# Two-layer decoder on one core: fp32 foldings and ternary weights moved late, expert lanes moved, the experts' product turned, fewer products for bias and sums

## The reference, cut to what matters

```python
# layer 0
x = ln(x + (einsum('bes,st->bet', x, Wr + Wc) + bias))            # a mix over the last axis, with decay matrices
x = ln(x + cross_attention(x, ctx, Wq, Wkv_expand, Wout))
logits = x @ router_w; e = argmax(logits)                         # one of 8 experts for each token
xs = x * sigmoid(max(logits))
x = ln(x + (silu(xs @ gate_w[e]) * (xs @ up_w[e])) @ down_w[e] + shared_ffn(x))
# layer 1
x = ln(x + fft_attention(x, W_q, W_kv, W_o))
q_big = ((x @ Wq.T) per head) @ w_kc_q;  q_r = q_big @ W_qr;  k_r = kv_rope @ W_kr     # 16 heads
out = (softmax(q_r k_r) kv_rope @ w_kc_kv.T) @ Wo.T
x = ln(x + out)
gu = x @ ternary(w_gate_up).T; h = silu(gate) * up                # 2 x 1024 columns
x = ln(x + rms_norm(h) @ ternary(w_proj).T)
```

## Time and profile before

| | us |
|---|---|
| median of 3 runs (lowest, highest) | 703.32 (700.88, 707.11) |
| the profiled execution's own time | 706.16 |
| its span (first to last instruction) | 704.9 |
| instructions | 14612 |

### The profile page before, as it was taken

How to read it: one execution, slowest core, us unless ns; L and a number is a source line. 1 busy time by engine, 2 the same in 40 slices (tenths; PEclk the granted TensorE clock), 3 DMA queues, 4 the chain that set the end, 5 groups by cost and what they waited for, 6 DMA issues and landing times.

```text
span 704.9 us, 14612 instructions
## 1 busy us (share of the span) xinstructions
PE 595.1 (84%) x5393; PEld 460.6 (65%) x5393; DVE 503.4 (71%) x1297; ACT 408.1 (58%) x914; POOL 357.3 (51%) x405
## 2 busy tenths in 40 slices
PE   4888788998898775899267789999989999999996
PEld 3655566776666553555233578888768777978885
DVE  3766557776787787556279867777888879968475
ACT  2765456665677752444173356666675766578374
POOL 2435665765549870000398933264484543245565
PEclk9998899999999898999767799999999999999999
DMA  7642212423023422231501000001101010000001
GB/s 235 191 150 75 71 43 85 113 81 99 24 76 124 135 96 90 90 99 61 153 27 45 16 1 2 1 1 32 31 1 31 1 31 3 1 1 2 1 1 61
DMA packets 50416, 41.98 MB, mean 60 GB/s; under 512 B 15513, under 2 KB 48794, under 8 KB 50330
## 3 DMA queue, kind: packets, MB, share of 16 engines
q1 hardware_dynamic: 48810, 36.85, 17.7%
q0 software_dynamic: 1536, 4.20, 1.8%
HBM read 31.72 MB, written 10.35 MB: 60 GB/s over the span
## 4 chain that ended last, share of the span: by engine, by line
PE 42%; DVE 7%; ACT 5%; issue 4%; POOL 2%; DMA 0%; POOLq 0%; DVEq 0%; ACTq 0%
PE bank L1032 8%; PE bank L1034 7%; PE bank L1033 7%; PE bank L1450 6%; PE bank L1039 4%; PE bank L1214 3%; DVE wide L1763 1%; ACT wide L1589 1%; PE bank L1432 1%; PE bank L1315 1%; PE bank L1290 1%; PE bank L1317 1%; PE bank L1288 1%; PE bank L1287 1%; PE bank L1286 1%
## 5 line engine op out<-in xcount | busy, mean ns | idle before, releaser
L1763 DVE TENSOR_TENSOR first<-bank,first 128x512 f16<-128x512 f32 (+3 forms) x113 | 65.3, 592 | 19.4 <-ACT first L1656 6.3
L1039 PE MATMUL bank<-c_identity,wide 128*128 128x128 f32 (+2 forms) x267 | 46.4, 295 | 34.3 <-ACT wide L1589 17.8
L2220 POOL TENSOR_TENSOR first<-first 128x512 f16<-128x512 f32 x44 | 53.0, 1208 | 37.6 <-ACT first L1650 32.4
L1039 PEld LDWEIGHTS bank<-c_identity,wide 128*128 128x128 f32 (+2 forms) x267 | 32.7, 149 | 42.7 <-ACT wide L1589 19.2
L1763 DVE TENSOR_TENSOR wide<-bank,wide 128x512 f16<-128x512 f32 (+3 forms) x85 | 47.0, 566 | 16.1 <-ACT wide L1629 8.5
L1039 PE MATMUL bank<-c_identity,first 128*128 128x128 f32 (+2 forms) x297 | 48.2, 285 | 7.7 <-DVE first L1949 2.4
L2244 POOL DMA_INDIRECT wide<-made_rows,made_at x8 | 8.1, 1007 | 75.3 <-DMA made_rows<-wide 73.5
L1039 PEld LDWEIGHTS bank<-c_identity,first 128*128 128x128 f32 (+2 forms) x297 | 33.7, 140 | 15.3 <-DVE first L1949 3.0
L2200 POOL TENSOR_TENSOR first<-first,minus_half 128x2 f32<-128x2 f32 x30 | 21.5, 717 | 27.8 <-DVE first L1872 27.8
L1032 PE MATMUL bank<-wide,first 128*128 128x256 f16 (+3 forms) x115 | 28.1, 260 | 7.2 <-DVE first L1763 5.9
L2319 POOL TENSOR_TENSOR wide<-wide 128x512 f16<-128x512 f32 x16 | 18.0, 1124 | 31.2 <-ACT wide L1739 31.2
(11 more groups left out here) (509 smaller groups left out, 2249.0 us busy)
## 6 DMA issues: line engine op xcount, KB each, us to landing
wide<-in_L_xattn_Wq SPq DMA_DIRECT2D x9, 256.0 KB, 3.1
wide<-in_L_ffn_gate_w SPq DMA_DIRECT2D x8, 256.0 KB
wide<-in_L_ffn_up_w SPq DMA_DIRECT2D x8, 256.0 KB
wide<-in_L_ffn_down_w SPq DMA_DIRECT2D x8, 256.0 KB
wide<-in_L_xattn_Wo SPq DMA_DIRECT2D x16, 128.0 KB
wide<-in_L_ffn_w_gate_up SPq DMA_DIRECT2D x8, 256.0 KB
first<-in_x SPq DMA_DIRECT2D x7, 256.0 KB, 5.0
x_mid<-first SPq DMA_DIRECT2D x7, 256.0 KB, 3.2
```

Of the source, the lines that this page charges most:

```text
L1039: last = nc.tensor.transpose(view[0:m, c0:c0 + n], src, kc["identity" if dt == F32 else "identity_bf"][0:n, 0:n])
L1763: return V.tensor_tensor(lo, whole, hi, ALU.subtract)
L2220: G.tensor_tensor(B.pl[r], B.pf, B.ph[r], ALU.subtract).then_inc(says("ex_l"), 1)
```

## The change

1. `TURNS` is now e0 to e2, h0 to h3, e3 to e7, h4 to h7, and then the ternary stages in the order 0, 4, 1, 5, 2, 6, 3, 7. A unit of layer 1 waits for less at a time: `q` g for folding 2g + 1, `gu` g for stages g and g + 4, `proj` 2 and 3 for all.
2. The expert lanes leave the staging buffers: lanes 0 to 2 lie over layer 0's lane 3, lane 3 over the fifth, lanes 4 to 6 over lane 0. Each waits for the store of the unit that was there (`was_in`). The shared experts' weights and the layer 1 lanes move or shrink to make room.
3. `x_gu` takes the expert's weights as the stationary operand in blocks of 128 columns, so that gate and up come out turned, and `x_b`'s transposes go. `x_b_hi` and `x_b_lo` read `X.h` in SBUF.
4. The bias is one product of 128 rows instead of two of one row (`pm_b` prepares two rows, the rest zero). `rm` needs two products instead of four, since `ss` of the last group adds the two halves on POOL.
5. A folding: `hb` writes its two heads to output rows 0 to 63 and 64 to 127, head by head in turn; `hk` is one transpose, and `hc` two products with a block-diagonal `krT` instead of four.

```diff
-TURNS = [("e", e) for e in range(KEPT)] + [(kind, n) for n in range(NPREP) for kind in "hf"] + [("e", e) for e in range(KEPT, NE)]
+EARLY_FOLDS = 4
+TERNARY = [n // 2 + 4 * (n % 2) for n in range(NPREP)]
+TURNS = ([("e", e) for e in range(KEPT)] + [("h", n) for n in range(EARLY_FOLDS)] + [("e", e) for e in range(KEPT, NE)]
+         + [("h", n) for n in range(EARLY_FOLDS, NPREP)] + [("f", n) for n in TERNARY])
+def was_in(n):
+    return 3 if n < 3 else 4 if n == 3 else FIRST
...
-        if n < LANES:
-            gate += prepared
-        elif o is None:
-            gate += [("in_mid", FIRST - 2, 0), ("in_mid", FIRST - 1, 0)]
+        if o is None:
+            gate += [("in_mid", was_in(n), 0)]
...
-        chain("x_b", n, 0, [("x_h", n, 0)], k, pe=32, hi=38, lo=42)
+        p.add("x_b_hi", n, 0, "ACT", 38, [("x_h", n, 0)], k)
+        p.add("x_b_lo", n, 0, "DVE", 40, [("x_b_hi", n, 0)], k)
...
-            chain("q", u, g, [("turn_lo", u, 1), ("ho_lo", 0, NPREP - 1)], k, pe=136)
+            chain("q", u, g, [("turn_lo", u, 1), ("ho_lo", 0, 2 * g + 1)], k, pe=136)
...
-            p.add("gu", u, g, "PE", 180, [("turn_lo", u, 2)] + [("fw_c", 0, i) for i in range(NPREP)], k, 2, ("hf", u, g))
+            p.add("gu", u, g, "PE", 180, [("turn_lo", u, 2)] + [("fw_c", 0, i) for i in (g, g + 4)], k, 2, ("hf", u, g))
...
-        a = wide.back(stage_at + n * 5120) if n < LANES else fifth.back(6144) if n == LANES else couples[1].back(LANE0 + (n - LANES - 1) * 5120)
+        a = couples[1].back(LANE0 + n * 5120) if n < 3 else fifth.back(6144) if n == 3 else couples[0].back((n - 4) * 5120)
...
-        for n in range(HEADS):
-            for q in range(2):
-                last = mm(b[0:R, n * D:(n + 1) * D], W.qr[:, q, n, :], k.t1[:, n, q, :], start=(q == 0), stop=(q == 1))
+        for q in range(2):
+            for n in range(HEADS):
+                last = mm(b[n * R:(n + 1) * R, 0:D], W.qr[:, q, n, :], k.t1[:, n, q, :], start=(q == 0), stop=(q == 1))
...
-            for n in range(HEADS):
-                mm(b[:, (2 * c + n) * DC:(2 * c + n + 1) * DC], k.t2[:, n * D + c * P:n * D + (c + 1) * P], k.krT[:, n * DC:(n + 1) * DC],
-                   start=True, stop=True)
+            mm(b[:, c * P:(c + 1) * P], k.t2[:, c * P:(c + 1) * P], k.krT, start=True, stop=True)
...
-                    for half in range(2):
-                        last = mm(o, kc["all_ones"][0:1, :], k.bias[half], start=False, stop=(half == 1))
+                    last = mm(o, kc["all_ones"], k.bias, start=False, stop=True)
...
-        for c in range(C):
-            last = mm3(b[:, :], cut(X.xT, ALL, slice(c * P, (c + 1) * P)), tuple(w[:, c * 2 * D:(c + 1) * 2 * D] for w in gu), c == 0, c == C - 1)
+        for m in range(2 * C):
+            for c in range(C):
+                at = c * 2 * D + m * P
+                last = mm3(b[:, m * P:(m + 1) * P], tuple(w[:, at:at + P] for w in gu), cut(X.xT, ALL, slice(c * P, (c + 1) * P)), c == 0, c == C - 1)
...
-            for n in range(2):
-                last = mm(b[:, t:t + 1], B.ss[:, n * S + t * P:n * S + (t + 1) * P], k.one, start=(n == 0), stop=(n == 1))
+            last = mm(b[:, t:t + 1], B.ss[:, t * P:(t + 1) * P], k.one, start=True, stop=True)
...
+        if g == 3:
+            pool.step(last)
+            last = G.tensor_tensor(B.ss[:, 0:S], B.ss[:, 0:S], B.ss[:, S:2 * S], ALU.add)
```

More of the change, by code:

```diff
@@ L141 @@
               "fold_dve": ("hq_lo", "ho_lo"), "ternary_dve": ("f_sc", "f_gt"), "route_dve": ("rt_top", "rt_hot", "rk_seen", "rk_slot"), "gate_act": ("rt_gate", "rt_xs"), "table_dve": ("tb_cnt", "tb_tile", "tb_tok"),
-              "expert_pe": ("x_t", "x_gu", "x_b", "x_dn"), "expert_act": ("x_t_hi", "x_tan", "x_b_hi", "x_out"),
+              "expert_pe": ("x_t", "x_gu", "x_dn"), "expert_act": ("x_t_hi", "x_tan", "x_b_hi", "x_out"),
               "expert_dve": ("x_t_lo", "x_h", "x_b_lo")}
@@ L655, in program @@
     k.t1 = wide.tile([HEADS, 2, D], F32, 96)
[L656 removed]
+    k.t2 = wide.tile([D])
     k.t3 = wide.tile([2 * D])
[L658 removed]
+    k.krT = sb("krT", [P, P])[:]
     wide_end = wide.at
@@ L668, in program @@
     pre.dv = wide.tile([2])
-    pre.bias = wide.tile([S], F32, 1)
+    pre.bias, pre.rest = wide.tile([S], F32, 2), wide.tile([S], F32, 2)
     pre.ones32 = wide.tile([P])
@@ L758, in tile @@
             raise AssertionError("no room")
-        area = tile([4608])
+        area = tile([4096])
         def part(at, words, dt=F32):
@@ L860, in ld_mix @@
         load(pre.wrow, A["L0_attn_weight"][1:2, :].broadcast_to([P, S]), dma["mix"])
-        load(pre.bias, A["L0_attn_bias"].rearrange("(a n) -> a n", a=1), dma["mix"])
+        load(pre.bias, A["L0_attn_bias"].rearrange("(a n) -> a n", a=1).broadcast_to([2, S]), dma["mix"])
         for c in range(C):
@@ L1096, in hk @@
         W = k.W[k.stage_no["h", j] % 2]
-        flip(bank("hk", 0, j), [(n * DC, R, W.kr[:, n, :]) for n in range(HEADS)]).then_inc(says("hk"), 1)
+        flip(bank("hk", 0, j), [(0, P, W.kr.rearrange("p h n -> p (h n)"))]).then_inc(says("hk"), 1)
     def ha(u, j):
@@ L1208, in proj @@
         else:
+            for i in range(NPREP):
+                pe.wait_ge(*done("fw_c", 0, i))
             b = bank("proj", u, n)
@@ L1441, in gu @@
         pe.wait_ge(*done("turn_lo", u, 2))
-        for i in range(NPREP):
+        for i in (g, g + 4):
             pe.wait_ge(*done("fw_c", 0, i))
@@ L1464, in tensor_program @@
     parts = {f.__name__: f for f in (pm_mm, pt, pd, po, pb, hk, ha, hw, hb, hc, fw, turn, ctx, kv, proj, q, max, mt, sc, pv, ot, rt, rk, sh, tb,
-                                     x_t, x_gu, x_b, x_dn, ft, kt, cs, vt, gu, rm)}
+                                     x_t, x_gu, x_dn, ft, kt, cs, vt, gu, rm)}
     for name, u, g in k.plan.order["PE"]:
@@ L1542, in hk_c @@
         act.wait_ge(*done("hk", 0, j))
-        fn(k.krT, bank("hk", 0, j)[0:R, 0:HEADS * DC], ACT.Copy).then_inc(says("hk_c"), 1)
+        act.wait_ge(*done("pm_pow", 0))
+        for n in range(HEADS):
+            own = slice(n * R, (n + 1) * R)
+            last = fn(k.krT[own, n * DC:(n + 1) * DC], bank("hk", 0, j)[own, 0:DC], ACT.Copy)
+        last.then_inc(says("hk_c"), 1)
     def ha_c(u, j):
@@ L1556, in hb_c @@
         act.wait_ge(*done("hb", 0, j))
-        fn(k.t2, bank("hb", 0, j)[0:R, :], ACT.Copy).then_inc(says("hb_c"), 1)
+        fn(k.t2, bank("hb", 0, j)[:, 0:D], ACT.Copy).then_inc(says("hb_c"), 1)
     def hq_hi(u, j):
@@ L1692, in x_b_hi @@
     def x_b_hi(n, g):
-        act.wait_ge(*done("x_b", n))
-        fn(k.X[n % ELANES].hT[0], bank("x_b", n)[:, 0:D], ACT.Copy).then_inc(says("x_b_hi"), 1)
+        act.wait_ge(*done("x_h", n))
+        fn(k.X[n % ELANES].hT[0], k.X[n % ELANES].h, ACT.Copy).then_inc(says("x_b_hi"), 1)
     def x_out(n, g):
@@ L2095, in x_b_lo @@
         dve.wait_ge(*done("x_b_hi", n))
-        rest(X.hT[1], bank("x_b", n)[:, 0:D], X.hT[0]).then_inc(says("x_b_lo"), 1)
+        rest(X.hT[1], X.h, X.hT[0]).then_inc(says("x_b_lo"), 1)
     def kt_lo(u, g):
@@ L2187, in pm_b @@
     def pm_b(u, g):
-        pool.step(G.tensor_copy(k.bias[0], pre.bias))
-        G.tensor_tensor(k.bias[1], pre.bias, k.bias[0], ALU.subtract).then_inc(says("pm_b"), 1)
+        rows = k.bias[0:2, :]
+        pool.step(G.memset(k.bias, 0.0))
+        pool.step(G.tensor_copy(rows, pre.bias))
+        pool.step(G.tensor_scalar(pre.rest, rows, kc["identity"][0:2, 1:2], None, ALU.mult))
+        G.tensor_tensor(rows, pre.bias, pre.rest, ALU.subtract).then_inc(says("pm_b"), 1)
     def eg_lo(u, e):
```

61 lines of the change are left out of this document (26 added, 35 removed).

## The result

The changed kernel takes 699.22 us in the median of 20 runs (696.29 to 705.76), the kernel before 703.34 us in runs beside them (700.88 to 708.43). The ratio is 0.9944, 95% interval 0.9917 to 0.9971: 4 us less, where the prediction had 26. The changed kernel's profiled span is 695.0 us against 704.9.

A forecast was written before the change was run, and what follows sets the result against it. PE was taken as the bound in three stretches, with two holes between. Layer 0 -32, experts +9, layer 1 -3 made -26 on 706.16, 680.2; the median, 2.8 lower, was given as 677.5, range 661 to 699.

The forecast's parts named there:

- the cover: Experts and nearby holes: late foldings and ternary stages fit idle time at no cost; static work runs under address steps.
- Layer 0: -32 forecast: Layer 0: foldings and ternary stages leave, foldings and bias get cheaper; 37.2 us of PE, taken as 32, ends 38 and 12.
- four foldings of 6.6 us: Layer 0: four foldings go from before to after e3 to e7, taking 26.4 us of PE out of the stretch.
- The lanes rival: Layer 0 is bound by its lanes, not PE: it shortens by only 12 us, giving 697.5; chance 0.13.
- Late stages at nothing: Ternary stages behind the experts: their 52 us of POOL meet 73 us of idle POOL, so cost nothing.
- Wrong would be ternary steps after 370: A sign against the forecast: ternary steps still running later than 370 us in the profile.
- the collision rival: Late stages hold up gathers, tiles or layer 1's first units: +13 us, giving 690.5; chance 0.13.
- The experts at +9: Experts' stretch: address steps make a tile 3.2 us, the stretch 82 us instead of 73; ends -3 and +41.
- the static work, folds included, runs under the steps: Experts' stretch: PE work at fixed places, foldings included, is hidden under the address steps.
- The hidden-steps rival: Experts: the sequencer runs ahead and hides the address steps; they gain 3 us instead of losing 9, giving 665.5; chance 0.15.
- the stalled array: Experts' turned product: each of 24 weight loads needs its own unhidden step, 5.5 us a tile, +53 us, 730; chance 0.09.
- Layer 1 at -3: Layer 1: halved `rm` saves 4 us; a second `ss` addition, on the last unit's chain only, costs about 0.7.

The follow-up runs named there:

- k18: k16 with `TURNS` as before, so foldings and ternary stages in the old turns, re-laid; 710.57 us, ratio 1.0096 to the kernel before.
- k7: Changed kernel, same order, with the ternary arithmetic on DVE and POOL cut to 1 of its 12 groups a row; 695.17 us, ratio 0.9835.
- k16: k6 with five early foldings and 24 passes of `settle`, re-laid; 681.57 us, ratio 0.9675.
- k5: Changed kernel with `rm` and `ss` as before, in program and plan, re-laid; 714.97 us, ratio 1.0139.
- k15: Changed kernel's same work, re-laid with `x_gu` told to the plan as 1.39 us; 713.37 us, ratio 1.0119.
- k8: Kernel before, same order, with the ternary arithmetic on DVE and POOL cut to 1 of its 12 groups a row; 689.85 us, ratio 0.978.
- k3: Changed kernel, same order, with gate and up weights of a fixed expert (tile number modulo 8), so no address steps in `x_gu`; 688.32 us, ratio 0.9757.
- k1: Changed kernel with the experts' product and `x_b` as before, re-laid; 698.57 us, ratio 0.9932.
- k6: k1 with `rm` and `ss` as before and six foldings instead of four ahead of experts 3 to 7; 695.23 us, ratio 0.9833.
- k17: k16 with the turned product and without `x_b`'s transposes; 705.04 us, ratio 1.0001.
- k2: Kernel before with the turned product and without `x_b`, re-laid; 729.31 us, ratio 1.0344.
- k4: Changed kernel with `TURNS` as before, re-laid; 739.87 us, ratio 1.0477.
- k10: Kernel before, same order, with `rm` of two products and the second addition in the last `ss`, program only; 706.08 us, ratio 1.0018.
- k9: Changed kernel, same order, with `rm`'s four products back and the last group's single addition, program only; 698.88 us, ratio 0.9906.
- k13: Kernel before's same work, re-laid with `x_gu` told to the plan as 1.30 us instead of 1.37; 719.34 us, ratio 1.0225.

## Why the prediction was wrong, step by step

The step that failed is the cover: the late stages costed at nothing, and the static work that was to run under the address steps. The experts' stage grew by 24.1 us instead of 9, and layer 1 by 9.3 instead of falling by 3. Layer 0's larger gain hid part of it, and came in another way than forecast.

**Layer 0: -32 forecast, -43.3 measured: the sign right, the mechanism only in part.** The prices of the folding were right: eight matmuls of `hb` and four of `hc` in the changed kernel,

```profile
241.06 1.08 PE L1121 MATMUL bank<-wide 96*64 96x256 f32 x8
246.12 0.68 PE L1129 MATMUL bank<-krT,wide 128*128 128x128 f32 x4
```

and `hb` in the kernel before:

```profile
45.63 1.94 PE L1120 MATMUL bank<-wide 96*64 96x256 f32 x8
```

`hb` saves 0.86 (0.97 forecast), `hc` 0.42 of 1.1 (0.4). But the largest term, four foldings of 6.6 us that leave the stretch, did not come about. `hb` of the changed kernel between 191 and 226 us:

```profile
L1121 PE MATMUL bank<-wide x24: 378/380/431, 197.9 to 223.4; 96*64 96x256 f32 x24
```

These 24 are three of the four late foldings. They run behind e3 to e7 as laid, but ahead of the first `x_gu` at 232.6; only the last folding runs behind it. What leaves or gets cheaper is then one folding, seven times 1.5 us, the bias and the transposes, about 22 us, an estimate from the forecast's own prices.

The second thing is the clock, which the forecast weighed only in the hole before unit 8. The busy time of PE from the start to the first `x_gu`, in the kernel before, the changed kernel and k18 (columns as in the earlier trace rows; the granted clock is 0.92, 0.96 and 0.87):

```profile
0.00:275.90 275.90, 220.21 (x2238) 165.09 (x2238) 193.04 (x495) 163.49 (x376) 158.78 (x157) 0.92 0.36 105
```

```profile
0.00:232.60 232.60, 186.48 (x2106) 144.69 (x2106) 159.28 (x442) 147.44 (x353) 108.11 (x128) 0.96 0.37 111
```

```profile
0.00:282.20 282.20, 214.07 (x2183) 160.27 (x2183) 186.45 (x496) 163.07 (x385) 160.10 (x160) 0.87 0.35 103
```

The trace grants either 1.2 or 2.4 GHz. The table divides PE's busy time by that (us):

| stretch | kernel | length | PE busy | of it at 1.2 GHz | PE idle |
|---|---|---|---|---|---|
| to the first `x_gu` | before | 275.9 | 220.2 | 36.1 | 55.7 |
| | changed | 232.6 | 186.5 | 14.3 | 46.1 |
| | k7 | 240.0 | 192.3 | 28.0 | 47.7 |
| | k18 | 282.2 | 214.1 | 56.7 | 68.1 |
| | k16 | 226.2 | 188.9 | 17.2 | 37.3 |
| unit 8 to the end | before | 348.1 | 316.9 | 25.8 | 31.2 |
| | changed | 357.4 | 314.4 | 20.2 | 43.0 |
| | k5 | 375.7 | 325.1 | 36.0 | 50.6 |
| | k15 | 371.0 | 324.8 | 39.0 | 46.2 |

If work at 1.2 GHz counts by half, the rest is its length at the full clock, an estimate. It gives 179.3 us for the changed kernel and 178.3 for k7, whose program and order are the same in this stretch, though one took 7.4 us longer, so the count holds there. Layer 0's 43.3 us are then 22.9 us of work (202.2 to 179.3), 10.8 of clock and 9.6 of idle time. The busy time fell by 33.7, close to the 37.2 forecast, but that nearness is luck.

The lanes rival's 12 us are refuted. But PE did not set the rate alone, as k8's 15.5 us show, which come from DVE and POOL. With the old turns the cheaper folding, the bias and new lanes gave nothing in layer 0 (k18: 282.2 against 275.9): by the same count work falls by 16.5 us, and the clock (10.3) and idle time (12.4) take more than that back. From k18 to k16 the late turns then gain 56 us, of which only 5 are work, 20 are clock and 31 idle time. The move paid, by a way that the forecast had not. The rows show idle time and the low clock together; no run separates which led.

**Late stages at nothing: wrong.** This step failed by reading capacity where latency decides. I set 52 us of POOL against its 73 idle us. But the stages run through two buffers. The last row of each kind, from the changed kernel: the ternary transposes on PE, and POOL's step 1 of two stages in a row with its wait,

```profile
L1040 PE MATMUL bank<-c_identity_bf,wide x48: 216/219/220, 261.8 to 411.7; 128*128 128x128 bf16 x48
```

```profile
264.56 1.75 POOL L2261 TENSOR_TENSOR wide<-wide 128x768 bf16<-128x768 bf16 x1 [7.10 <-DVE wide L1860]
...
278.08 1.75 POOL L2261 TENSOR_TENSOR wide<-wide 128x768 bf16<-128x768 bf16 x1 [6.72 <-DVE wide L1860]
```

A stage follows the last one after 13.5 us, with POOL idle for 7 of them. (That it is the two buffers and not the fixed order that set this pace is read from the times below; no run had a third buffer.) The loads for the stage begun at 278 were issued at 263, its rounding on ACT ran at 271.7, DVE was done at 278.0, POOL at 284.8, its transposes came at about 291. With the first transposes at 262, the eighth stage's can't come before 262 + 7 x 13.5 = 356, and the gathers of layer 1 come at 324. Six stages had all but one of POOL's steps before the gathers; the rest fell on layer 1, the last transposes at 411.7. "Wrong would be ternary steps after 370" was the sign, and it came true. The price of the late arithmetic with the order held is k7's 7.7 us. This is the collision rival's mechanism (13 us by the forecast, chance 0.13).

**The experts at +9, +24.1 measured: the step that failed most.** The row behind it was right, as the loads above show: 2.0 us for 16 address steps. What failed is "the static work, folds included, runs under the steps" and the sum of 3.2 us a tile, and with it the late stages at nothing. In the 83 us from the first `x_gu` to the end of the last, PE's waits in the changed kernel are few:

```profile
PE bank L1033 <- issue: 6.1, 16, 0.7
PE bank L1033 <- DVE first L1764: 3.9, 4, 1.4
```

So the engine is occupied, not waiting. By the starts of the matmuls `x_gu` holds PE for 46.4 us (before 29.9), `x_dn` 13.4, `x_t` 6.3, the late foldings 4.1; the timeline has no other load between the 24 of a product. A tile is then the sum of its products, 66 / 23 = 2.9, with 0.2 to 0.3 for the late work and about 0.45 of idle time, some 3.6 us against 3.69 between readings; I had let `x_t` count 0.05 and the folding nothing. The 0.49 us more a tile make 11 of the 15 us missed. The other 4 are idle time at the stage's ends, which I let shrink by 5 and which stayed (22.8 us of the stage lie outside the readings before, 23.9 now).

k3 divides the stage. By the forecast the steps were worth 12 us (-3 to +9); with them gone and the order held, the stage falls by 10.2, so their price was about right. What the forecast lacked is the rest: without steps it had the stage 3 us shorter than before, and k3 has it 13.9 longer. PE is busy 62.9 us in it against 58.0, with one late folding of 4.1 in it, and idle 31.9 against 22.8. k7 puts 2.3 us of this stage on the ternary arithmetic. k1, with the old product, still has 10.0 more than before; k16 has 5.3 and k6 22.0, in other orders and with more early foldings. Which share each has stays open.

Re-laid pairs give the turned product +25 (k17 to k16, k2 to before) and +31 (k4 to k18, `rm` with it) in the span; the changed kernel against k1 gives -3. In the experts' stage all four agree in sign: 14.7, 18.1, 22.5, 14.1. The hidden-steps rival is refuted; so is the stalled array, which would need a tile of over 4.5 us. (The term's upper end of +41 was a wrong sum: that rival's own 53 us on top of +9 are +62.)

The Trainium skill ("TensorE: Matmul & The Clock Gate", Back-to-back issue gap) gives 81 ns a matmul for 128 columns. k3's row of the same product at fixed places shows 55 ns, so the trace does not agree here either, and it isn't this rule that made the product long.

**Layer 1 at -3: wrong sign, +9.3 measured.** `rm` lost nearly half (4.3 us against 7.9 of PE), but I put the second addition "on the chain of the last unit only". It stands in each unit's chain, k10 shows 3.9 us more of waiting for it, and with the order held the halved `rm` costs 1 to 3 us (k10, k9), both within their intervals. By the table on the clock, work in layer 1 is the same as before (304.0 and 304.2 us at the full clock), the clock gives 2.8 us, and 11.8 us of idle time are new. Which share the late stages (k7) and the order have of these stays open: k4, with every stage early, is 359.4 long, k9 360.3, and re-layings of the kernel before reach 357.6 without any change.

**The order as a term.** The prediction had none for it. Three orders of the kernel before's work span 1.0000 to 1.0225, four of the changed work 0.9939 to 1.0177. Lowest against lowest is -0.6%, mean against mean -0.8%. That is small beside the spread of 2%, so the 4 us belong to these two orders, and seven orders do not show that the edits as a whole are worth them. Single terms of 3 us can't be read from re-laid kernels either. The large ones can with care, and they nearly cancel: by k16, k17 and k18, late turns -31 us, the turned product +25; the pair of the changed kernel and k1, with -3, is the exception for the product.

Part of this spread is the clock. In the 20 runs of the changed kernel the mean granted clock runs from 0.957 (696.29 us) to 0.934 (705.76), about 4 us for 0.01. The medians are 0.949 for it and 0.937 for the kernel before, so by an estimate from that slope its better clock is worth some 5 us, as much as its whole gain. Of layer 1's 18.3 us more in k5, 7.9 are clock, 7.6 idle time and 2.9 work; of the 13.6 in k15, 9.4 are clock. But k13 has the clock of the kernel before (0.935 both) and is 14 us slower, so the order acts by idle time too.

Since 699.22 lies at the edge, the range of 661 to 699 did not hold it. Six of the 22 us missing are the two profiled executions, each 3 us from its median, the changed one under and the one before over it; in the profiles the miss is 16: +15 in the experts, +12 in layer 1, -11 in layer 0.

## What to carry to other kernels

Before work is moved into an idle engine's time, lay one item's whole chain (load, each engine, buffer free again) against the gap: the number of buffers and the chain's length say how many items fit, not the engine's idle sum. Look up where an item will run, too: a part laid late may still come before the mark that it was to leave. Compare PE's busy time only with the granted clock beside it. Where operands are addressed from a register, count distinct addresses, not matmuls, and charge them in full, with what stands behind; here a product of few wide streams beat one of many narrow ones in three pairs of four, though it costs two transposes. Where a planner writes the order, re-lay both kernels a few times before an edit under 2% is judged, and take the best version from the spread.
